# A gated cross-attention block with routed experts on one core: a projection's products spread between an attention slot's scores

## The chip, the cores and the metric

The kernel runs on one core of a Trainium2 chip, as one launch. The metric is the device time in microseconds. Before the change three runs took 877.08, 871.36 and 870.76 us (median 871.36 us).

## The reference

`x` is (8, 256, 512), eight batches of 256 tokens; `ctx` has the same shape. Everything is float32. Cut to what matters:

```
h  = layernorm(x)
q  = concat(ctx, h) @ Wq                      # 32 heads of 16
k  = h @ Wk ; v = h @ Wv ; sk = ctx @ Wsk ; sv = ctx @ Wsv      # 8 key heads of 16
scores = q @ concat(sk, k)^T / 4 + alibi,  banded to 64 keys back, softmax
x  = x + tanh(g0) * (softmax(scores) @ concat(sv, v)) @ Wo
h2 = layernorm(x)
x  = x + tanh(g1) * (routed experts of h2, top 4 of 128, mixed from 8 bases, + a shared expert)
```

The attention is 256 units of work: 8 batches, 8 key heads, 4 blocks of 64 queries. A unit's scores are computed twice: once with queries as rows, for the maxima of the softmax, and once turned, with keys as rows, for the probabilities that multiply the values.

## The kernel before

Each product of two float32 matrices is made of three fp32r products (high times high, low times high, high times low). The splitting into high and low parts is done by ScalarE (ACT, the high part) and then by VectorE (DVE) or GpSimd (POOL), the low part.

**Slots.** PE's program for the attention is a loop over slots, `for n in range(SLOTS)`, written out by hand. A batch has 32 slots, and "slot 24" here means n mod 32 = 24. In slot n PE does, in this order:

- `scores(n)` (L1944): two products with 114 rows, `ps_scores<-k_stack,q_stack`, of 192 columns each, or of 128 each in every fourth unit. DVE reduces them to maxima (`neg_max`, L1490). Before it starts, the unit two slots back must have been reduced (semaphore `max_done`).
- in every eighth slot `times_v` (L1987, 64 instructions on PE with a 32-column weight load each), in another of eight `turn_max` (L1962), a turning of the maxima.
- `scores_turned(n - 18)` (L1973): two products with 116 rows and 256 columns, `ps_scoresT<-q_stack,k_stack` (one in every fourth unit). ACT takes the exponentials (`probsT`, L1128). Before it starts, the unit two slots back must be through ACT (`exp_done`).
- turnings of normalised rows, in some slots.
- **a piece of a projection** for a later batch, in 24 of a batch's 32 slots: a third of a key, value or query projection (8 products of 128 rows and 256 columns) or of an output projection `times_wo` (4 products of 128 rows and 512 columns). In the first eight slots it is an eighth of a query projection (3 products).
- in the last batches and behind them: router, gate and up products of the expert part.

Which slot has which piece comes from tables at the top: `K_PROJ`, `V_PROJ`, `Q_PROJ`, `EARLY_Q` and `TIMES_WO`. Over the whole loop 167 slots have a piece: 18 of keys, 21 of values, 86 of queries (8 of them of three products), 42 of the output. The output projection of a batch starts in slot 24 of the next batch (batches 0 to 5), that of batch 6 in slot 25 of the last one.

**Waits around a piece.** The first product of a projection waits until its PSUM bank has been emptied (`take_bank`, `pj_done`). For the output projection it waits for more: `oT_lo`, the low part of the attention's output. That comes about so: `times_v` on PE; DVE turns and inverts; POOL multiplies; DVE turns back (`oT_raw`); ACT makes `oT_hi` (L1139); POOL makes `oT_lo` (L847). The last `oT_hi` of a batch stands in ACT's order directly behind the exponentials of slot 22, and slot 22 has the last third of a value projection.

ACT, DVE and POOL work through lists of their own, each strictly in order.

## Time and profile before

| | |
|---|---|
| runs | 877.08, 871.36, 870.76 us |
| the profiled execution: time | 872.62 us |
| its span | 870.6 us |
| PE busy | 858.4 us, 99% of the span |
| weight loads (PEld) busy | 753.4 us, 87% |
| DVE, POOL, ACT busy | 545.2, 519.9, 399.3 us |
| granted TensorE clock | 1.00 in every stretch asked for |
| chain that ended last | PE 84%, POOL 10%, DMA 2%, DVE 2% |

PE is TensorE's matmuls, PEld its weight loads, which have a row of their own. The profile models where a matmul ends, and consecutive matmuls overlap in it, so the distance between starts is what a product costs. The attention runs from about 34 us to about 400 us; the shared and routed experts follow and end the program.

### The profile page before, as it was taken

The page shows a single profiled execution, that of the slowest core. Times are in us where ns is not written, and L with a number is a line of the kernel's source. Part 1 is how long each engine was busy: PE and PEld are TensorE (multiplying, and loading weights), DVE is VectorE, ACT ScalarE, POOL GpSimd, SP SyncE. Part 2 cuts the span into 40 slices and gives each one's busy share as a digit, 9 for nine tenths or more (in the row PEclk, how much of TensorE's full clock was granted, in tenths as well). Part 3 has the DMA queues.
Part 4 walks back from the last instruction along what each step waited for, and adds up shares of the span by engine and source line. Part 5 has one row for each costly group of instructions (what it writes and reads, how often), then busy time and mean ns, then how long its engine had stood idle before and what let it go on. Part 6 is the DMA issues. An engine that isn't in the chain of part 4 may idle for free.

```text
span 870.6 us, 17391 instructions
## 1 busy us (share of the span) xinstructions
PE 858.4 (99%) x6662; PEld 753.4 (87%) x6662; DVE 545.2 (63%) x984; ACT 399.3 (46%) x807; POOL 519.9 (60%) x532
## 2 busy tenths in 40 slices
PE   9899999999999999999999999999999999999998
PEld 8889999999999998988888877888888888888886
DVE  7675666766666657756446756556655655665567
ACT  5754545554545544655035243444444444444431
POOL 3861443535335232343769998548888887888641
PEclk9999999999999999999999999999999999999999
DMA  8678676776868659630101354320212022021046
GB/s 275 170 143 180 152 207 186 191 196 167 205 165 218 163 139 256 144 100 25 49 25 49 102 168 157 134 73 25 82 40 73 25 72 73 25 84 38 1 151 236
DMA packets 76509, 108.09 MB, mean 124 GB/s; under 512 B 7274, under 2 KB 47979, under 8 KB 75403
## 3 DMA queue, kind: packets, MB, share of 16 engines
q1 hardware_dynamic: 74168, 105.94, 43.4%
q10 hardware_dynamic: 2258, 1.03, 0.5%
q8 instruction: 54, 0.88, 0.5%
q14 instruction: 29, 0.23, 0.1%
HBM read 70.71 MB, written 31.00 MB: 117 GB/s over the span
## 4 chain that ended last, share of the span: by engine, by line
PE 84%; POOL 10%; DMA 2%; DVE 2%; issue 1%; SPq 1%; ACT 0%; POOLq 0%; ACTq 0%
PE ps_scores L2227 20%; PE ps_proj L1846 15%; PE ps_scoresT L2227 10%; PE ps_scoresT L1983 7%; PE ps_o L1997 6%; PE ps_scores L1956 5%; PE ps_proj L2227 5%; PE ps_proj L1904 5%; PE ps_scores L1846 3%; PE ps_proj L1835 3%; PE ps_scoresT L1846 1%; DMA q_stack<-max_rows 1%; POOL sum_lo L953 1%; POOL sum_raw L968 1%; POOL sum_raw L966 1%; DMA xn_rows<-in_x 1%
## 5 line engine op out<-in xcount | busy, mean ns | idle before, releaser
L1128 ACT ACTIVATE probsT<-ps_scoresT 128x512 f32<-128x512 f32 (+1 forms) x256 | 138.9, 545 | 148.9 <-PE ps_scoresT L1983 144.4
L1490 DVE TENSOR_REDUCE neg_max<-ps_scores 128x2 f32<-128x384 f32 (+1 forms) x256 | 131.6, 516 | 108.6 <-PE ps_scores L1956 107.8
L1357 ACT ACTIVATE part_sums<-ps_scores 128x512 f32<-128x512 f32 x96 | 57.4, 598 | 130.1 <-PE ps_scores L2227 130.0
L1983 PE MATMUL ps_scoresT<-q_stack,k_stack 116*128 116x256 f32 x448 | 106.1, 307 | 0.8 <-DMA q_stack<-max_rows 0.8
L841 POOL TENSOR_TENSOR o_normal<-o_blocks,inv_sums 128x256 f32<-128x256 f32 x32 | 19.9, 622 | 138.0 <-DVE inv_sums L1511 138.0
L1956 PE MATMUL ps_scores<-k_stack,q_stack 114*128 114x192 f32 (+1 forms) x512 | 94.5, 267 | 2.7 <-DMA q_stack<-qT_hi 1.6
L1956 PEld LDWEIGHTS ps_scores<-k_stack,q_stack 114*128 114x128 f32 x512 | 83.0, 190 | 9.5 <-DMA q_stack<-qT_hi 2.3
L996 POOL TENSOR_TENSOR w_expert_lo<-w_sums,w_expert_hi 128x256 fp32r<-128x256 f32 x64 | 64.2, 1014 | 44.9 <-ACT w_expert_hi L1277 44.9
L1008 POOL TENSOR_TENSOR big<-big,basis 128x512 f32<-128x512 f32 x56 | 77.9, 1409 | 16.3 <-DVE basis L1785 16.3
L1983 PEld LDWEIGHTS ps_scoresT<-q_stack,k_stack 116*128 116x128 f32 x448 | 70.8, 190 | 4.7 <-DMA q_stack<-max_rows 1.0
L1776 DVE TENSOR_TENSOR basis<-part_sums,silu_gate 128x512 f32<-128x512 f32 x32 | 24.2, 755 | 67.3 <-ACT silu_gate L1365 67.3
L1846 PE MATMUL ps_proj<-actT_hi,wq_hi 128*128 128x256 f32 x224 | 63.6, 284 | 0.5 <-DVE second_qT_lo L1467 0.5
L1846 PE MATMUL ps_proj<-actT_lo,wq_hi 128*128 128x256 f32 x224 | 63.3, 282 | 0.0
L1846 PE MATMUL ps_proj<-actT_hi,wq_lo 128*128 128x256 f32 x224 | 63.3, 282 | 0.0
L847 POOL TENSOR_TENSOR oT_lo<-oT_raw,oT_hi 128x256 fp32r<-128x256 f32 x32 | 23.6, 737 | 59.0 <-ACT oT_hi L1139 59.0
L1785 DVE TENSOR_TENSOR basis<-basis,big 128x512 f32<-128x512 f32 x56 | 56.8, 1015 | 1.0
L1997 PE MATMUL ps_o<-probsT,v_ones 128*32 128x128 f32 (+1 forms) x2048 | 55.7, 261 | 0.0
L1755 DVE TENSOR_TENSOR part_sums<-part_sums,ps_scoresT 128x512 f32<-128x512 f32 x32 | 22.0, 687 | 53.4 <-ACT part_sums L1357 53.4
L1997 PEld LDWEIGHTS ps_o<-probsT,v_ones 128*32 128x32 f32 x2048 | 50.5, 110 | 4.0 <-issue 1.1
L996 POOL TENSOR_TENSOR w_expert_lo<-w_raw,w_expert_hi 128x256 fp32r<-128x256 f32 x48 | 46.4, 980 | 6.9 <-ACT w_expert_hi L1277 6.8
L2227 PE MATMUL ps_scores<-xnT_hi,w_expert_hi 128*128 128x512 f32 x128 | 49.8, 389 | 0.0
L2227 PE MATMUL ps_scores<-xnT_hi,w_expert_lo 128*128 128x512 f32 x128 | 49.8, 389 | 0.0
(309 smaller groups left out, 2500.9 us busy)
## 6 DMA issues: line engine op xcount, KB each, us to landing
k_stack<-k_kept SPq DMA_DIRECT2D x64, 192.0 KB, 4.3
big<-coeff_rows SPq DMA_DIRECT2D x8, 1024.0 KB, 4.8
q_stack<-q_kept SPq DMA_DIRECT2D x40, 192.0 KB, 4.1
q_kept<-qT_hi SPq DMA_DIRECT2D x10, 512.0 KB
x_rows<-in_x SPq DMA_DIRECT2D x9, 512.0 KB, 5.8
k_kept<-kT_hi SPq DMA_DIRECT2D x16, 256.0 KB
x_kept<-x_rows SPq DMA_DIRECT2D x16, 256.0 KB, 2.6
w_raw<-in_L_ffn_w_gate SPq DMA_DIRECT2D x16, 256.0 KB, 2.8
```

The lines of the kernel that those rows point to most:

```text
L996: pool.tensor_tensor(WS[n % 2]["lo"][:, w, :], w_source(n, w), WS[n % 2]["hi"][:, w, :].bitcast(F32), ALU.subtract).then_inc(e_lo, 1)
L1008: pool.tensor_tensor(dst, dst, BS[:, j, :], ALU.add).then_inc(acc_done, 1)
L1128: act.activation(PT[:, g % 2, 2 * j:2 * j + blocks].rearrange("p h f r w -> p (h f r w)"), ST[:, n % 2, 0:blocks].rearrange("p h n -> p (h ...
L1357: act.activation(TP[:, u % 2, j, :], src[:, u % 2, :], ACT.Copy).then_inc(taken, 1)
L1490: dve.tensor_reduce(NM[:, g // 2 % 2, g % 2, 2 * i:2 * i + 2], SA[:, n % 2, :, 0:keys], AX.X, ALU.max, negate=True).then_inc(max_done, 1)
L1785: dve.tensor_tensor(dst, BS[:, j, :], cB[:, k % 2, group_columns(t)], ALU.mult).then_inc(basis_done, 1)
L1846: ins = pe.matmul(out, stat(s, c), mov(m, c), start=i == 0, stop=i == len(steps) - 1, skip_group_check=True)
L1904: ins = pe.matmul(dst[:, src * T:(src + 1) * T], WKV[w][:, m + src, c, :], AT[x][:, src * HC + c, :], start=i == 0, stop=i == HC * PARTS - ...
L1956: ins = pe.matmul(SA[:, n % 2, f, 0:2 * (near.stop - near.start)], QS[0:TOP, g, i, f].rearrange("p r w -> p (r w)"), keys[:, near, :].rear ...
L1983: ins = pe.matmul(ST[:, n % 2, v, :], KS[0:ROWS, g, j + v, 1 - v].rearrange("p w s -> p (w s)"), QS[0:ROWS, g, j + v].rearrange("p f r w - ...
L1997: ins = pe.matmul(POB[32 * r:32 * r + 2 * D, n % 2, j * W:j * W + cols_j], VA[:, j, n % HK, :], PT[:, n % 2, 2 * j:2 * j + cols_j // W, :, ...
L2227: ins = pe.matmul(bank[:, u % 2, :], WS[n % 2][s][:, w, c * P:(c + 1) * P], operand(MEETS[w], m, c, g), start=first and c == 0 and j == 0, ...
```

## The change

The piece of a projection no longer stands behind the slot's scores as one block. `scores` and `scores_turned` each do one of their two products per call, and a new function `projected(n, cut)` does a part of the slot's piece: its first product between the two score products, its second before the turned scores, its third between the two turned ones, and the rest where the piece stood before. Slots without a piece keep their order. Nothing is added or taken away, and the lists of ACT, DVE, POOL and SyncE stay as they are.

```diff
-        def third(out, stat, mov, count, part, pieces=3):
+        def third(out, stat, mov, count, part, done, pieces=3, cut=WHOLE):
             steps = [(c, s, m) for c in range(count) for s, m in PASSES]
             size = len(steps) // pieces
-            for i in range(part * size, (part + 1) * size) if part is not None else range(len(steps)):
+            piece = range(part * size, (part + 1) * size) if part is not None else range(len(steps))
+            for i in piece[cut]:
                 c, s, m = steps[i]
                 ins = pe.matmul(out, stat(s, c), mov(m, c), start=i == 0, stop=i == len(steps) - 1, skip_group_check=True)
-            return ins
+                if i == len(steps) - 1:
+                    ins.then_inc(done, 1)
...
-        def times_wo(b, t, part):
-            first = part in (0, None)
+        def times_wo(b, t, part, cut=WHOLE):
+            first = part in (0, None) and cut.start == 0
             dst = take_bank("wo", b, t) if first else place("wo", b, t)
             if first:
                 pe.wait_ge(oT_lo, HC * (b + 1))
                 banks_back(b)
-            ins = third(dst, lambda h, c: OT[h][:, t, c, :], lambda h, c: WO[h][:, c, :], HC, part)
-            if part in (2, None):
-                ins.then_inc(wo_mm, 1)
+            third(dst, lambda h, c: OT[h][:, t, c, :], lambda h, c: WO[h][:, c, :], HC, part, wo_mm, cut=cut)
...
+        def projected(n, cut):
+            if n < PIECES:
+                queries(1, 1, n, PIECES, cut)
+            for part in range(3):
+                b = due(n, K_PROJ[part], 2)
+                if b is not None:
+                    keys_values_third("k", b, part, cut)
...
         for n in range(SLOTS):
             if n < END:
-                scores(n)
+                scores(n, 0)
+            projected(n, slice(0, 1))
+            if n < END:
+                scores(n, 1)
             p = pair_due(n, PV)
             if p is not None:
                 times_v(p)
             p = pair_due(n, NM_TURN)
             if p is not None:
                 turn_max(p)
+            projected(n, slice(1, 2))
             if LAG <= n < END + LAG:
-                scores_turned(n - LAG)
+                scores_turned(n - LAG, 0)
+            projected(n, slice(2, 3))
+            if LAG <= n < END + LAG:
+                scores_turned(n - LAG, 1)
...
+            projected(n, slice(3, None))
```

The waits stand at the same products as before, `max_done` at a slot's first score product and `exp_done` at its first turned one; the semaphores that tell that a pair is done are raised by the second. In the rows below `ps_proj` is the projection's bank, and what stands in brackets is what the instruction waits for.

PE in slot 22, the last third of a value projection, before:

```order
L1956 MATMUL ps_scores<-k_stack,q_stack 128x192 [waits max_done]
L1956 MATMUL ps_scores<-k_stack,q_stack 128x192
L1983 MATMUL ps_scoresT<-q_stack,k_stack 128x256 [waits exp_done]
L1983 MATMUL ps_scoresT<-q_stack,k_stack 128x256
L1904 MATMUL ps_proj<-actT_hi,wkv_lo 128x256
L1904 MATMUL ps_proj<-actT_lo,wkv_hi 128x256
```

and now:

```order
L1957 MATMUL ps_scores<-k_stack,q_stack 128x192 [waits max_done]
L1907 MATMUL ps_proj<-actT_hi,wkv_lo 128x256
L1957 MATMUL ps_scores<-k_stack,q_stack 128x192
L1907 MATMUL ps_proj<-actT_lo,wkv_hi 128x256
L1986 MATMUL ps_scoresT<-q_stack,k_stack 128x256 [waits exp_done]
L1907 MATMUL ps_proj<-actT_hi,wkv_hi 128x256
L1986 MATMUL ps_scoresT<-q_stack,k_stack 128x256
L1907 MATMUL ps_proj<-actT_hi,wkv_lo 128x256
L1907 MATMUL ps_proj<-actT_lo,wkv_hi 128x256
```

The second turned product now stands behind three products of the piece; five instead of eight follow it.

PE in slot 24, where an output projection starts, before:

```order
L1956 MATMUL ps_scores<-k_stack,q_stack 128x128 [waits max_done,q_in6,stack_in6]
L1956 MATMUL ps_scores<-k_stack,q_stack 128x128
L1983 MATMUL ps_scoresT<-q_stack,k_stack 128x256 [waits exp_done]
L1983 MATMUL ps_scoresT<-q_stack,k_stack 128x256
L1846 MATMUL ps_proj<-wo_hi,oT_hi 128x512 [waits oT_lo,pj_done]
L1846 MATMUL ps_proj<-wo_hi,oT_lo 128x512
```

and now:

```order
L1957 MATMUL ps_scores<-k_stack,q_stack 128x128 [waits max_done,q_in6,stack_in6]
L1848 MATMUL ps_proj<-wo_hi,oT_hi 128x512 [waits oT_lo,pj_done]
L1957 MATMUL ps_scores<-k_stack,q_stack 128x128
L1848 MATMUL ps_proj<-wo_hi,oT_lo 128x512
L1986 MATMUL ps_scoresT<-q_stack,k_stack 128x256 [waits exp_done]
L1848 MATMUL ps_proj<-wo_lo,oT_hi 128x512
L1986 MATMUL ps_scoresT<-q_stack,k_stack 128x256
L1848 MATMUL ps_proj<-wo_hi,oT_hi 128x512
```

The product that waits for `oT_lo` has moved ahead of three of the slot's four score products.

## Rows read from the trace of the kernel before

**Rows 1.** Stretch (us), busy of PE, PEld, DVE, ACT, POOL, granted clock, DMA share, GB/s.

```profile
200.00:300.00 100.00, 100.00 (x1185) 95.84 (x1184) 70.28 (x161) 52.26 (x108) 43.02 (x56) 1.00 0.74 190
```

**Rows 2.** Waits of PE, the longest in total: us, times, longest.

```profile
PE ps_scores L1956 <- DMA q_stack<-qT_hi: 1.6, 3, 0.6
```

**Rows 3.** Timeline, weight loads (PEld), one slot: start us, us, instruction.

```profile
303.37 0.31 PEld L1956 LDWEIGHTS ps_scores<-k_stack,q_stack 114*128 114x128 f32 x2
...
303.60 0.30 PEld L1983 LDWEIGHTS ps_scoresT<-q_stack,k_stack 116*128 116x128 f32 x2
...
303.83 0.19 PEld L1846 LDWEIGHTS ps_proj<-actT_hi,wq_hi 128*128 128x128 f32 x1
...
304.79 0.31 PEld L1956 LDWEIGHTS ps_scores<-k_stack,q_stack 114*128 114x128 f32 x2
```

**Rows 4.** Timeline, matmuls (PE) of two score pairs.

```profile
303.49 0.37 PE L1956 MATMUL ps_scores<-k_stack,q_stack 114*128 114x192 f32 x2
...
304.78 0.28 PE L1846 MATMUL ps_proj<-actT_hi,wq_lo 128*128 128x256 f32 x1
...
304.90 0.34 PE L1956 MATMUL ps_scores<-k_stack,q_stack 114*128 114x128 f32 x2
```

**Rows 5.** Timeline, the end of slot 22 and slot 24 of one batch.

```profile
144.12 0.30 PEld L1983 LDWEIGHTS ps_scoresT<-q_stack,k_stack 116*128 116x128 f32 x2
...
144.67 0.60 ACT L1128 ACTIVATE probsT<-ps_scoresT 128x512 f32<-128x512 f32 x1 [0.24 <-PE ps_scoresT L1983]
...
145.17 0.41 ACT L1139 ACTIVATE oT_hi<-oT_raw 128x256 fp32r<-128x256 f32 x1
...
145.65 0.74 POOL L847 TENSOR_TENSOR oT_lo<-oT_raw,oT_hi 128x256 fp32r<-128x256 f32 x1 [2.68 <-ACT oT_hi L1139]
...
146.22 0.30 PEld L1956 LDWEIGHTS ps_scores<-k_stack,q_stack 114*128 114x128 f32 x2
...
146.68 0.19 PEld L1846 LDWEIGHTS ps_proj<-wo_hi,oT_hi 128*128 128x128 f32 x1
```

**Rows 6.** Timeline, the first such place.

```profile
99.19 0.73 POOL L847 TENSOR_TENSOR oT_lo<-oT_raw,oT_hi 128x256 fp32r<-128x256 f32 x1 [2.78 <-ACT oT_hi L1139]
...
99.66 0.30 PEld L1956 LDWEIGHTS ps_scores<-k_stack,q_stack 114*128 114x128 f32 x2
```

**Rows 7.** Timeline, the last such place.

```profile
330.99 0.73 POOL L847 TENSOR_TENSOR oT_lo<-oT_raw,oT_hi 128x256 fp32r<-128x256 f32 x1 [2.69 <-ACT oT_hi L1139]
...
331.56 0.30 PEld L1956 LDWEIGHTS ps_scores<-k_stack,q_stack 114*128 114x128 f32 x2
```

**Rows 8.** Timeline, a projection whose first load waits for POOL.

```profile
63.57 1.28 POOL L834 TENSOR_TENSOR actT_lo<-ctx_turned,actT_hi 128x512 fp32r<-128x512 f32 x1
...
64.96 0.19 PEld L1904 LDWEIGHTS ps_proj<-actT_hi,wkv_hi 128*128 128x128 f32 x1
```

**Rows 9.** Timeline, slot 9 of the first batch.

```profile
41.37 0.41 DVE L1467 TENSOR_TENSOR second_qT_lo<-ps_proj,second_qT_hi 128x256 fp32r<-128x256 f32 x1
...
41.84 0.19 PEld L1846 LDWEIGHTS ps_proj<-actT_hi,wq_hi 128*128 128x128 f32 x1 [0.72 <-DVE second_qT_lo L1467]
```

**Rows 10.** Timeline, slot 25 of the last batch.

```profile
371.35 0.30 PEld L1956 LDWEIGHTS ps_scores<-k_stack,q_stack 114*128 114x128 f32 x2
...
371.49 0.59 ACT L1157 ACTIVATE logitsT<-ps_proj 128x512 f32<-128x512 f32 x1
...
372.08 0.09 PEld L1971 LDWEIGHTS ps_scoresT<-ident,max_halves 128*32 128x32 f32 x1 [0.43 <-DVE max_halves L1500]
...
372.28 0.19 PEld L1846 LDWEIGHTS ps_proj<-wo_hi,oT_hi 128*128 128x128 f32 x1
...
373.08 0.43 PEld L1956 LDWEIGHTS ps_scores<-k_stack,q_stack 114*128 114x128 f32 x2
```

**Rows 11.** Timeline, a close wait of a turned score.

```profile
233.71 0.60 ACT L1128 ACTIVATE probsT<-ps_scoresT 128x512 f32<-128x512 f32 x1 [1.92 <-PE ps_scoresT L1983]
...
234.53 0.30 PEld L1983 LDWEIGHTS ps_scoresT<-q_stack,k_stack 116*128 116x128 f32 x2
```

More of the change, by code:

```diff
@@ L78 @@
 LAG = 18
+WHOLE = slice(0, None)
 PAIR = 2 * NB
@@ L2105, in _ @@
         queries(1, 0, 1, 2)
+        def projected(n, cut):
[5 more added lines that the diff above has]
+                    keys_values_third("k", b, part, cut)
+                for r in range(G):
+                    b = queries_due(n, r, part)
+                    if b is not None and (b > 1 or r > 1):
+                        queries(b, r, part, cut=cut)
+                b = due(n, V_PROJ[part], 1)
+                if b is not None:
+                    keys_values_third("v", b, part, cut)
+                for t in range(TB):
+                    b = wo_due(n, t, part)
+                    if b is not None:
+                        if b == 0 and t == 0 and part == 0 and cut.start == 0:
+                            for m in range(FIRST_O, len(halves)):
+                                wait_split(pe, m)
+                        times_wo(b, t, part, cut)
         for n in range(SLOTS):
             if n < END:
-                scores(n)
+                scores(n, 0)
+            projected(n, slice(0, 1))
+            if n < END:
+                scores(n, 1)
             p = pair_due(n, PV)
```

81 lines of the change are left out of this document (28 added, 53 removed).

## The prediction

> **What bounds the kernel now.** I read the share of busy time first: PE is busy for 858.4 of 870.6 us. Then the stretches. From 200 to 300 us, in the middle of the attention, PE has no idle time at all and the granted clock is 1.00, that is 2.4 GHz, while the next engine, DVE, is at 70% [rows 1]. Then PE's own waits: the longest in total is 1.6 us in three waits, for the first loads of the query stack [rows 2], and all its other waits are shorter in total. So the attention is bound by the number of products on PE and by what each costs there. Time is gained only if a product becomes cheaper; it is lost wherever PE is made to wait, since nothing later gives it back.
>
> What a product costs is read from the starts of the weight loads, since the profile models the ends of matmuls. In one slot the loads of two scores, two turned scores and eight projection products start at 303.37, 303.49, 303.60, 303.71 and 303.83, and those of the next slot at 304.79 (a merged pair's second start is its end less 0.19) [rows 3]. A load starts with the matmul before it, so the cost of one shows one place late: 303.60 - 303.49 and 303.71 - 303.60 are the two scores, 0.11 us each, 303.83 - 303.71 a turned product, 0.12, and (304.79 - 303.83) / 8 a projection product, 0.12: 2 x 0.11 + 2 x 0.12 + 8 x 0.12 = 1.42 us, which is 304.79 - 303.37.
>
> **The order alone: 0.** In 167 slots the same products change places. The score product is the only one whose columns need less than its cost: its pair starts 0.09 us apart with 192 columns and 0.06 with 128 (0.37 and 0.34 less 0.28, the length of a single matmul) [rows 4], yet the loads behind it are 0.11 apart [rows 3]. So what a score costs is the weight load of whatever comes next, and a projection product's load is the same 0.19 us long. I take each product's cost to be its own, whoever its neighbours are: the sum above has three changes of kind in it and nothing left over. Bounds: it could save 0.02 us per wide score and 0.05 per narrow one, or lose what a reading can hide, 0.01 us per change of kind; both are rivals below. I take 0 because the sum of the twelve closes with nothing over.
>
> The Trainium skill, "TensorE: Matmul & The Clock Gate", on what happens when a matmul is issued, says that the next tile's weights load while this tile's matmul runs. Taken alone it speaks for the change: a wide product beside a narrow one hides its load. The trace agrees only that far, that the load starts with the matmul before it, and its 0.11 us stand behind a 0.06 us matmul; by the rule the sum would be the first rival's, by the row it is 0.
>
> **What moves earlier and waits.** The first product of a piece is now second in its slot, ahead of one score and two turned ones: 0.11 + 0.12 + 0.12 = 0.35 us earlier. Query, key and value pieces wait there only for a bank emptied microseconds ago; PE shows no wait at them in the stretch without idle [rows 1]. The output projection waits for `oT_lo`, and there it is tight. **What moves later** is the second turned product, by three products, 0.36 us, and with it ACT's exponentials. In slot 22 they start at 144.67, directly behind their release, ACT having been idle; `oT_hi` follows at 145.17 directly behind them, and `oT_lo` on POOL, which had waited 2.68 us, from 145.65 to 146.39 [rows 5]. All three move by 0.36 us, since none had slack: `oT_lo` ends at 146.75. Slot 22 holds the last third of a value projection in all six batches concerned. In slot 24 the scores' load starts at 146.22, the output product could load at 146.33, and before loaded at 146.68 [rows 5]. What such a wait takes from POOL's end to the load is seen elsewhere: `actT_lo` ends at 64.85 and the load starts at 64.96, 0.11 us [rows 8]. So the load starts at 146.75 + 0.11 = 146.86, and PE waits 0.53 us. In the first such place POOL ends at 99.92 and the scores load at 99.66: 99.92 + 0.36 + 0.11 - 99.77 = 0.62 [rows 6]. In the last it is 331.72 + 0.47 - 331.67 = 0.52 [rows 7]. Four more lie between, like the one shown: 0.62 + 4 x 0.53 + 0.52 = **3.3 us**. Bounds per place: 0.17 us if `oT_lo` does not move, 0.53 if all of it does; I take the second because ACT and POOL both stood waiting.
>
> **Two smaller places.** In slot 9 of the first batch the piece waits for DVE's `second_qT_lo`, which ends at 41.78; the load follows at 41.84 [rows 9]. A score product (0.11) and the turning of the maxima (0.09, the length of its load [rows 10]) were done inside that wait and now come behind it: +0.2 us. In slot 25 of the last batch the output projection also waits for ACT's `logitsT`, which ends at 372.08, so it loads at 372.19. Behind it now come four output products (0.80, from 372.28 to 373.08 before) and three that had been ahead, 0.11 + 0.09 + 0.12: slot 26 starts at 373.31 instead of 373.08 [rows 10]: +0.2 us.
>
> **What gets more room.** The first turned product of a slot moves 0.24 us later, or more behind output products. Its closest wait in the steady part is in slot 20, where ACT ends at 234.31 and the load starts at 234.53 [rows 11]; it gains distance. But there was no wait there, so that is worth nothing. The longest waits, for DMAs of the query stack, stand at a slot's first score, which stays first.
>
> **Sum.** 3.3 + 0.2 + 0.2 = 3.7 us. Against the profiled execution's 872.62 us that gives 876.3. It stands 1.3 us over the median of the runs; against the median, 871.36, the forecast is **875.1 us**, 0.4% slower. The expert part gives little back: it runs on PE too, and no wait of PE as long as the longest one [rows 2] stands there.
>
> **Rivals.**
> 1. *Loads are hidden.* A score between two wide products costs only its columns: 0.02 us saved for each score in three of four units and 0.05 in the fourth, times two, times 167: 9.2 us. With the waits it is 9.2 - 3.7 = 5.5 us faster, 865.9; without them 862.2. For it: the load starts with the matmul before, and that is now a wide one. Against: it is the load behind the score that costs, and that one cannot start before the score does. Chance 0.10.
> 2. *The change does nothing to be seen.* The order costs nothing and `oT_lo` comes in time, because ACT's exponentials or POOL have slack that the trace hides, or what is lost at the output is won in the waits of the first and last batch: 871.4. For it: PE is idle for 870.6 - 858.4 = 12.2 us in all, and some of its waits now have products beside them. Against: the longest stand at a slot's first score [rows 2], which nothing of the slot can precede. Chance 0.17.
> 3. *Changing the height of the operands costs* (slower). Scores use 114 rows, turned ones 116, projections 128. A piece slot had three changes of height and now has eight: 5 x 167 = 835 more. At 0.01 us, the most that the intervals can hide, 8.4 us, and with the waits 12.1: 883.5. It passes 1% from 0.006 us a change. For it: no row shows a turned product directly behind a projection product. Against: the sum of twelve closes with three such changes in it. Chance 0.13.
>
> **Numbers.** The forecast has 0.60. About 1% (8.7 us) is what a measurement of this kernel can tell from no change; the three runs shown are 6.3 us apart. Over 1% faster is only the far end of rival 1, 0.04; over 1% slower is rival 3 and a little of the forecast's upper tail, 0.12; within 1%: 0.84. The range is 870.0 to 880.5: it takes in rival 2 with a microsecond of scatter, the forecast, and rival 3 with a price of up to 0.006 us, and leaves out rival 1 and the rest of rival 3.
>
> **What would show it.** PE's waits should have a new line, an output product waiting for POOL's `oT_lo`, six times with about 0.4 to 0.6 us each (less in that view, which counts from the modelled end of the matmul before). The slot of rows 3 should still take 1.42 us from its first load to the next slot's; 1.37 would be rival 1, 1.47 rival 3. The exponentials of slot 22 should start 0.36 us later after the slot's start than now. From the first such place to the last, five batches, 331.56 - 99.66 = 231.9 us pass now [rows 6, 7]; it should be 2.7 us more, 234.6. The prediction is wrong if no such wait stands in slot 24, or if the slots without it have a new length.

## Result, and the profile after

| | before | changed |
|---|---|---|
| median | 871.30 us (15 runs, 870.51 to 877.08) | 877.02 us (15 runs, 875.96 to 881.30) |
| ratio, 95% interval | | 1.007, 1.0057 to 1.0083 |
| profiled execution, span | 872.62, 870.6 us | 875.96, 873.9 us |

The change costs 5.7 us, 0.7%; 3.7 were forecast. The waits forecast are there in their places and sizes, and a small price that the prediction put at zero comes on top.

**The stretch without idle.** The changed kernel, same stretch and columns as [rows 1]:

```profile
200.00:300.00 100.00, 99.34 (x1183) 94.86 (x1176) 68.23 (x154) 51.38 (x107) 41.87 (x55) 1.00 0.70 183
```

PE was busy for 100.00 us here and now is for 99.34, at the same granted clock of 1.00: it waits.

**PE's waits.** The lines of the changed kernel's list (us in total, times, longest) that name one of the three places, and the DMA line of [rows 2]:

```profile
PE ps_proj L1848 <- POOL oT_lo L848: 2.1, 6, 0.4
PE ps_scores L1957 <- DMA q_stack<-qT_hi: 1.6, 3, 0.9
...
PE ps_proj L1848 <- DVE second_qT_lo L1468: 0.7, 1, 0.7
...
PE ps_proj L1848 <- ACT logitsT L1158: 0.5, 1, 0.5
```

An output product waits for `oT_lo` six times and has taken the top of the list. Before, neither the first nor the last of these lines was there. The view counts from the modelled end of the matmul before, so 2.1 us is less than the loss, as the prediction had said.

**Slots 22 and 24**, the same batch as [rows 5]: timeline of the changed kernel, start us, us, instruction, in brackets the idle time before it and its releaser.

```profile
146.38 0.60 ACT L1129 ACTIVATE probsT<-ps_scoresT 128x512 f32<-128x512 f32 x1 [0.61 <-PE ps_scoresT L1986]
...
146.88 0.41 ACT L1140 ACTIVATE oT_hi<-oT_raw 128x256 fp32r<-128x256 f32 x1
...
147.36 0.73 POOL L848 TENSOR_TENSOR oT_lo<-oT_raw,oT_hi 128x256 fp32r<-128x256 f32 x1 [3.06 <-ACT oT_hi L1140]
147.58 0.19 PEld L1957 LDWEIGHTS ps_scores<-k_stack,q_stack 114*128 114x128 f32 x1
...
148.21 0.19 PEld L1848 LDWEIGHTS ps_proj<-wo_hi,oT_hi 128*128 128x128 f32 x1 [0.44 <-issue]
```

Against slot 24's first load, the exponentials of slot 22 start 1.20 us ahead now (147.58 - 146.38) and did 1.55 us ahead before (146.22 - 144.67): 0.35 us later, forecast 0.36. `oT_hi` follows directly, `oT_lo` ends at 148.09, and 0.12 us behind that the output product loads. With no wait it would load one score product after 147.58, at 147.69, and loads at 148.21: 0.52 us lost, forecast 0.53.

The first and the last such place, as [rows 6] and [rows 7]:

```profile
100.04 0.73 POOL L848 TENSOR_TENSOR oT_lo<-oT_raw,oT_hi 128x256 fp32r<-128x256 f32 x1 [3.17 <-ACT oT_hi L1140]
100.17 0.19 PEld L1957 LDWEIGHTS ps_scores<-k_stack,q_stack 114*128 114x128 f32 x1
...
100.89 0.18 PEld L1848 LDWEIGHTS ps_proj<-wo_hi,oT_hi 128*128 128x128 f32 x1 [0.53 <-issue]
...
335.70 0.73 POOL L848 TENSOR_TENSOR oT_lo<-oT_raw,oT_hi 128x256 fp32r<-128x256 f32 x1 [3.08 <-ACT oT_hi L1140]
...
335.91 0.19 PEld L1957 LDWEIGHTS ps_scores<-k_stack,q_stack 114*128 114x128 f32 x1
...
336.54 0.19 PEld L1848 LDWEIGHTS ps_proj<-wo_hi,oT_hi 128*128 128x128 f32 x1 [0.44 <-issue]
```

The same reading gives 100.89 - 100.17 - 0.11 = 0.61 us and 336.54 - 335.91 - 0.11 = 0.52 us (forecast 0.62 and 0.52). From the first such place to the last, 235.74 us pass, and 231.90 before: 3.84 more, not 2.7. The waits are 2.7 of it (0.61 + 4 x 0.52). So something stands between the places.

**The slot of [rows 3].** Its first load and the next slot's in the changed kernel:

```profile
307.58 0.19 PEld L1957 LDWEIGHTS ps_scores<-k_stack,q_stack 114*128 114x128 f32 x1
...
309.01 0.19 PEld L1957 LDWEIGHTS ps_scores<-k_stack,q_stack 114*128 114x128 f32 x1
```

1.43 us, where 1.42 stood. That is at the edge of what two rows show. Over many slots it is not. I took the start of all 256 slots from both traces and subtracted their lengths. In ns, the fourth batch:

```
slots  0 to  7    1  18  -1  17   7   1  12  19
slots  8 to 15    8   3  -1  13   4  -1  -2   7
slots 16 to 23    3  17   0  -1   6  15  13   1
slots 24 to 31  517  11   5  12  15  -4   9  24
```

Slots without a piece (2, 9, 10, 13, 14, 18, 19, 23) keep their length within 3 ns. Those with one are longer by 10 ns on average, slot 24 left out, and by nearly the same amounts in each batch, slot by slot. Leaving slot 24 out, the six batches from the second to the seventh are longer by 258, 229, 231, 228, 231 and 229 ns: 1.4 us in all.

**The two smaller places**, slot 9 of the first batch as [rows 9], and slot 25 of the last as [rows 10]:

```profile
41.45 0.41 DVE L1468 TENSOR_TENSOR second_qT_lo<-ps_proj,second_qT_hi 128x256 fp32r<-128x256 f32 x1
41.91 0.19 PEld L1848 LDWEIGHTS ps_proj<-actT_hi,wq_hi 128*128 128x128 f32 x1 [0.88 <-DVE second_qT_lo L1468]
...
375.40 0.19 PEld L1957 LDWEIGHTS ps_scores<-k_stack,q_stack 114*128 114x128 f32 x1
...
375.54 0.59 ACT L1158 ACTIVATE logitsT<-ps_proj 128x512 f32<-128x512 f32 x1
...
376.25 0.19 PEld L1848 LDWEIGHTS ps_proj<-wo_hi,oT_hi 128*128 128x128 f32 x1 [0.66 <-issue]
...
377.38 0.43 PEld L1957 LDWEIGHTS ps_scores<-k_stack,q_stack 114*128 114x128 f32 x2
```

In slot 9 the load still follows DVE by 0.05 us, and the score and the turning now come behind it: the slot is 0.20 us longer, as forecast. In slot 25 ACT's `logitsT` ends at 376.13 and the load starts at 376.25; the slot takes 1.98 us instead of 1.73: 0.25, forecast 0.2.

**A wait that only the profile of before had.** Weight loads in the slot behind `times_v` at the start of the last batch, first before, then changed:

```profile
347.89 0.30 PEld L1983 LDWEIGHTS ps_scoresT<-q_stack,k_stack 116*128 116x128 f32 x2 [1.00 <-DMA q_stack<-max_rows]
```

```profile
351.92 0.30 PEld L1986 LDWEIGHTS ps_scoresT<-q_stack,k_stack 116*128 116x128 f32 x2
```

Before, PE had idled for 1.00 us for a DMA of the maxima; the changed kernel's execution has no such wait, and its slot is 0.89 us shorter. Whether that is scatter of one execution is not shown. Both profiles of before's order (before, e6) have the wait, all three of the full spread order (changed, e10, e5) lack it, and of the other experiments' profiles some have it and some don't. The budget below gives it apart.

**Budget of the two traces**, from the first slot's start to the last one's: 3.20 (six slots 24) + 0.20 + 0.25 + 1.41 (other slots with a piece, six batches) - 0.89 (the DMA wait) - 0.10 (the rest) = 4.07 us. Without that DMA wait it is 5.0.

### The profile page after: what moved, and what is told of

The parts are those of the page before. It is cut to its first block, busy times and chain, and to the rows that moved or that the text cites. A ratio compares the mean times of both kernels' runs of the same rounds, so it can differ in the third digit from the quotient of the medians.

```text
span 873.9 us, 17391 instructions
## 1 busy us (share of the span) xinstructions
PE 860.7 (98%) x6662; PEld 755.5 (86%) x6662; DVE 546.3 (63%) x984; ACT 398.1 (46%) x807; POOL 520.2 (60%) x532
## 4 chain that ended last, share of the span: by engine, by line
PE 81%; POOL 10%; issue 3%; DVE 3%; DMA 1%; ACT 1%; SPq 0%; POOLq 0%; DVEq 0%; ACTq 0%
PE ps_scores L2235 20%; PE ps_proj L1848 16%; PE ps_scoresT L2235 10%; PE ps_o L2001 6%; PE ps_scoresT L1986 6%; PE ps_proj L2235 5%; PE ps_scores L1957 4%; PE ps_proj L1907 3%; PE ps_scores L1848 3%; PE ps_proj L1836 3%; PE ps_scoresT L1848 1%; POOL sum_lo L954 1%; POOL sum_raw L969 1%; POOL sum_raw L967 1%; DMA xn_rows<-in_x 1%
## 5 line engine op out<-in xcount | busy, mean ns | idle before, releaser
L1957 PE MATMUL ps_scores<-k_stack,q_stack 114*128 114x192 f32 (+1 forms) x512 | 115.3, 258 | 2.7 <-DMA q_stack<-qT_hi 1.6
L1986 PE MATMUL ps_scoresT<-q_stack,k_stack 116*128 116x256 f32 x448 | 115.6, 295 | 0.0
L1957 PEld LDWEIGHTS ps_scores<-k_stack,q_stack 114*128 114x128 f32 x512 | 92.9, 191 | 6.9 <-DMA q_stack<-qT_hi 2.2
L1986 PEld LDWEIGHTS ps_scoresT<-q_stack,k_stack 116*128 116x128 f32 x448 | 80.0, 191 | 3.7
L1848 PE MATMUL ps_proj<-actT_hi,wq_hi 128*128 128x256 f32 x224 | 65.5, 292 | 0.7 <-DVE second_qT_lo L1468 0.7
L1848 PE MATMUL ps_proj<-actT_lo,wq_hi 128*128 128x256 f32 x224 | 65.4, 292 | 0.0
L1848 PE MATMUL ps_proj<-actT_hi,wq_lo 128*128 128x256 f32 x224 | 65.1, 291 | 0.0
L2235 PE MATMUL ps_scores<-xnT_lo,w_expert_hi 128*128 128x512 f32 x128 | 49.9, 390 | 0.0
```

Of the source, the lines that this page charges most:

```text
L1848: ins = pe.matmul(out, stat(s, c), mov(m, c), start=i == 0, stop=i == len(steps) - 1, skip_group_check=True)
L1957: ins = pe.matmul(SA[:, n % 2, f, 0:2 * (near.stop - near.start)], QS[0:TOP, g, i, f].rearrange("p r w -> p (r w)"), keys[:, near, :].rear ...
L1986: ins = pe.matmul(ST[:, n % 2, v, :], KS[0:ROWS, g, j + v, 1 - v].rearrange("p w s -> p (w s)"), QS[0:ROWS, g, j + v].rearrange("p f r w - ...
L2235: ins = pe.matmul(bank[:, u % 2, :], WS[n % 2][s][:, w, c * P:(c + 1) * P], operand(MEETS[w], m, c, g), start=first and c == 0 and j == 0, ...
```

## Experiments

One view decides between most theories. The distance from slot 24 of the third batch to slot 24 of the seventh is 185.34 us before [rows 5, 7] and has no waits of the start, the end or the DMA in it. It holds four places where `oT_lo` may be waited for and four batches of other slots. All were measured against before on the same chip.

| run | what it is | ratio, 95% interval | median, before | oT_lo, each of four | four batches, more than before |
|---|---|---|---|---|---|
| changed | | 1.007 (1.0057 to 1.0083) | 877.02, 871.30 | 0.52 | 2.99 |
| e1 | output pieces behind | 1.0048 (1.0028 to 1.0069) | 875.42, 871.95 | 0.17 | 1.31 |
| e2 | only output pieces spread | 1.0018 (1.0008 to 1.0028) | 873.72, 871.95 | 0.17 | 0.77 |
| e3 | as e1, slot 22's value piece behind | 1.0026 (1.0008 to 1.0044) | 874.30, 871.95 | 0 | 0.59 |
| e4 | oT_hi ahead of exponentials | 1.0024 (1.0008 to 1.0039) | 873.92, 871.95 | 0 | 0.96 |
| e5 | changed, all heights 114 | 1.0051 (1.0027 to 1.0074) | 876.62, 871.97 | 0.53 | 1.78 over e6 |
| e6 | before, all heights 114 | 1.0009 (0.9992 to 1.0025) | 871.92, 871.97 | 0 | 0.11 |
| e7 | only the two scores taken apart | 1.0042 (1.0025 to 1.0058) | 875.25, 871.97 | 0.28 | 1.57 |
| e8 | only the two turned ones apart | 1.0011 (0.9997 to 1.0025) | 873.05, 871.97 | 0.07 | 0.63 |
| e9 | changed, products of slots 0 to 33 behind | 1.006 (1.0039 to 1.0081) | 877.78, 871.68 | 0.52 | 3.01 |
| e10 | changed, again | 1.0057 (1.0036 to 1.0079) | 877.62, 871.68 | 0.52 | 3.02 |
| e11 | as e4 and e9, slot 25 of the last batch | 1.0035 (1.0021 to 1.0049) | 875.16, 871.68 | 0 | 0.96 |
| e12 | e11 without the moved waits | 1.0026 (1.0012 to 1.004) | 873.52, 871.97 | 0 | 0.96 |

**Which half of the wait is which: e1, e2, e3.** A wait for `oT_lo` has two causes, the product that moved ahead (slot 24) and the exponentials that moved back (slot 22). In e1 output pieces stay behind:

```diff
                 for t in range(TB):
-                    b = wo_due(n, t, part)
+                    b = wo_due(n, t, part) if cut.start == 3 else None
                     if b is not None:
...
-                        times_wo(b, t, part, cut)
+                        times_wo(b, t, part)
```

> The changed kernel with the output projection's pieces back behind the slot's scores; key, value and query pieces stay spread. Theory A (the loss is the wait for oT_lo, made of the product moved 0.35 us earlier and of oT_lo coming 0.36 us later, plus a price of about 9 ns a slot for the alternation): oT_lo still comes 0.36 us late, so a wait of about 0.18 us stays in five of the six places and 0.28 in the first, 1.2 us in place of 3.2; the alternation in the other 125 slots costs 1.1, slot 9 0.2: 2.5 us over the kernel before. Rival B (the wait comes from the earlier place alone): no wait for oT_lo at all, 1.3 us over. Rival C (the waits are given back later, and the loss is the alternation's): as slow as the changed kernel, 5 us over.

e2 is its mirror:

```diff
-            if n < PIECES:
+            wo_cut, cut = cut, (WHOLE if cut.start == 3 else slice(0, 0))
+            if n < PIECES and cut == WHOLE:
...
-                b = due(n, K_PROJ[part], 2)
+                b = due(n, K_PROJ[part], 2) if cut == WHOLE else None
...
-                        times_wo(b, t, part, cut)
+                        times_wo(b, t, part, wo_cut)
```

> Only the output projection's pieces are spread; key, value and query pieces stand behind the scores as before the change. Theory A: oT_lo comes as early as before the change, so the product moved 0.35 us ahead waits about 0.17 us in five places and 0.26 in the first, 1.1 us in all; slot 25 of the last batch costs 0.2, the alternation in 42 slots 0.4: 1.7 us over the kernel before. Rival B (the earlier place alone): the whole 3.2 us of waits, 3.9 us over. Rival C: 0.4 over.

e3 is e1 with the last third of a value projection (slot 22) whole as well:

```diff
-                if b is not None:
-                    keys_values_third("v", b, part, cut)
+                if b is not None and (part < 2 or cut.start == 3):
+                    keys_values_third("v", b, part, cut if part < 2 else WHOLE)
```

> As e1, and the last third of the value projection, in slot 22, also behind its scores. Theory A: oT_lo is on time and nothing asks for it earlier: no wait for it; what stays is the alternation in 118 slots, about 1.1 us, and slot 9, 0.2: 1.3 us over the kernel before, 1.2 under e1. Rival B: the same as its e1, as slot 22 doesn't matter.

Either half alone gives 0.17 us per place, both give 0.52, and without both it is 0 (slot 24 is 0 to 3 ns longer than before in e3). 0.17 + 0.17 is less than 0.52, because before the change `oT_lo` was early: in [rows 5] it ends at 146.39 and the product loads at 146.68, so, with the 0.11 us from POOL's end to the load, the first 0.18 us of either delay cost nothing. This is what the prediction's two bounds of 0.17 and 0.53 said. In the runs e1 and e3 stand further off than expected, e1 at +3.5 us for +2.5, e3 at +2.3 for +1.3; e2 is as expected. The last part of this section takes that up.

**Taking the wait away by ACT's order: e4.** The change stays whole; ACT makes a batch's last `oT_hi` ahead of slot 22's exponentials, which no longer delay it:

```diff
+            p = split_due(n)
+            if p is not None and p % HC == HC - 1:
+                o_high(p)
             if LAG <= n < END + LAG:
                 exponentials(n - LAG)
...
             p = split_due(n)
-            if p is not None:
+            if p is not None and p % HC < HC - 1:
                 o_high(p)
```

> The changed kernel with one step of ACT's list moved: the last oT_hi of a batch stands ahead of slot 22's exponentials instead of behind them. Theory A: the delay of the second turned product no longer reaches oT_lo, which ends about 0.7 us earlier than in the kernel before: all six waits for oT_lo go, 3.2 us under the changed kernel, 2.0 over the one before. Rival B' (POOL or DVE sets when oT_lo comes): the waits stay, no change against the changed kernel.

The same place in e4's timeline:

```profile
147.01 0.40 ACT L1140 ACTIVATE oT_hi<-oT_raw 128x256 fp32r<-128x256 f32 x1
...
147.49 0.74 POOL L848 TENSOR_TENSOR oT_lo<-oT_raw,oT_hi 128x256 fp32r<-128x256 f32 x1 [1.86 <-ACT oT_hi L1140]
...
147.72 0.60 ACT L1129 ACTIVATE probsT<-ps_scoresT 128x512 f32<-128x512 f32 x1 [0.30 <-PE ps_scoresT L1989]
...
148.92 0.19 PEld L1960 LDWEIGHTS ps_scores<-k_stack,q_stack 114*128 114x128 f32 x1
...
149.03 0.19 PEld L1851 LDWEIGHTS ps_proj<-wo_hi,oT_hi 128*128 128x128 f32 x1
```

`oT_lo` ends at 148.23, 0.8 us before the output product loads. That load comes 0.11 us behind the score's, with no wait; all six places are like this. e4 came out at +2.0 us as expected. It is the changed kernel's loss less the waits.

**Why slots with a piece are longer: e5 to e8.** Rival 3 had the height of the operands as its cause. In e5 and e6 every one of these products has 114 rows:

```diff
-                ins = pe.matmul(dst[:, src * T:(src + 1) * T], WKV[w][:, m + src, c, :], AT[x][:, src * HC + c, :],
+                ins = pe.matmul(dst[:, src * T:(src + 1) * T], WKV[w][0:TOP, m + src, c, :], AT[x][0:TOP, src * HC + c, :],
...
-                ins = pe.matmul(ST[:, n % 2, v, :], KS[0:ROWS, g, j + v, 1 - v].rearrange("p w s -> p (w s)"),
-                                QS[0:ROWS, g, j + v].rearrange("p f r w -> p (f r w)"), start=True, stop=True)
+                ins = pe.matmul(ST[:, n % 2, v, :], KS[0:TOP, g, j + v, 1 - v].rearrange("p w s -> p (w s)"),
+                                QS[0:TOP, g, j + v].rearrange("p f r w -> p (f r w)"), start=True, stop=True)
```

(and in the same way for query and output projections). Both kernels leave 14 of 128 terms out of every projection and the maxima out of the turned scores.

> The changed order with all operands of scores, turned scores and projections cut to 114 rows, so that no change of height is left between them. It leaves the maxima out of the turned scores and 14 of 128 terms out of every projection. To be read against e6, slot by slot. Theory H (the alternation's price, 8 to 23 ns in most slots with a piece, is that of changing height): slots of e5 are as long as those of e6, the waits aside. Rival L (it belongs to the alternation itself: another bank, another buffer): the same 5 to 23 ns stay.

> The order of the kernel before with the same cut to 114 rows; the same terms are left out. Both theories: as long as the kernel before within 0.5 us, since the height of an operand does not set how long its columns take.

The two loads that bound the four batches (slots 24 of the third and the seventh), first e6, then e5:

```profile
147.60 0.30 PEld L1956 LDWEIGHTS ps_scores<-k_stack,q_stack 114*128 114x128 f32 x2
...
333.05 0.30 PEld L1956 LDWEIGHTS ps_scores<-k_stack,q_stack 114*128 114x128 f32 x2
```

```profile
148.22 0.19 PEld L1957 LDWEIGHTS ps_scores<-k_stack,q_stack 114*128 114x128 f32 x1
...
335.45 0.19 PEld L1957 LDWEIGHTS ps_scores<-k_stack,q_stack 114*128 114x128 f32 x1
```

185.45 us and 187.23 us: 1.78 more. Four waits in slot 24 are 2.14 of it, so everything else is 0.36 us *shorter* with the products spread, where it was 0.92 us longer with unequal heights (2.99 - 4 x 0.517). In the fourth batch slots with a piece are from 16 ns shorter to 12 ns longer in e5 than in e6, nearly all of them shorter or equal. So the spread order costs something only where the heights are unequal. At equal heights it shows a small gain, some 4 ns a slot with a piece, in the direction of rival 1 at a thirteenth of its size (0.09 us a batch; it had 9.2 us over the eight). The runs are too coarse for either: e5's median is 4.7 us over e6's.

The other half of the comparison is e6 against before: the old order with the heights made equal, all changes of height between these products gone. Its four batches are 0.11 us *longer* than before's. A fixed price for each change of height would have made them shorter, by about 0.8 us at 2.2 ns each (my estimate from three changes in each of 24 slots and two in each of the other 8). So what costs is unequal heights in the spread order; the old order pays nothing for them.

e7 and e8 split the change by pair. e7 takes only the score products apart, e8 only the turned ones:

```diff
# e7
             projected(n, slice(0, 1))
...
-            projected(n, slice(1, 2))
             if LAG <= n < END + LAG:
                 scores_turned(n - LAG, 0)
-            projected(n, slice(2, 3))
...
-            projected(n, slice(3, None))
+            projected(n, slice(1, None))
```

> Only the two score products are taken apart: the first product of a piece between them, the rest behind the turned scores as before the change. Every piece's first product still moves 0.35 us earlier, the second turned product comes 0.12 us later. Theory A: a wait for oT_lo of 0.17 + 0.12 = 0.29 us in five places, 0.38 in the first, 1.8 us in all; slots get longer by what a projection product ahead of a single score costs. Theory P (the price sits at the turned pair, where the trace of the changed kernel shows 122 ns for a projection product ahead of a turned one and 121 ahead of a score, against 119): 1 to 3 ns a slot here and 3 to 8 in e8. Rival (it sits at the scores): the reverse.

```diff
# e8
-            projected(n, slice(0, 1))
...
-            projected(n, slice(1, 2))
             if LAG <= n < END + LAG:
                 scores_turned(n - LAG, 0)
-            projected(n, slice(2, 3))
+            projected(n, slice(0, 1))
...
-            projected(n, slice(3, None))
+            projected(n, slice(1, None))
```

> Only the two turned products are taken apart: the first product of a piece between them, the rest behind. The second turned product comes 0.12 us later, the first product of a piece 0.12 us earlier. Theory A: the product that waits for oT_lo is ready 0.12 us earlier and oT_lo comes 0.12 us later, against 0.18 us that are free after the 0.11 us a wait takes: waits of 0.06 us in five places and 0.15 in the first, 0.5 us in all; no cost in slot 9 beyond nothing, since no turned product stands there. Theory P: slots with a piece 3 to 8 ns longer.

Outside slot 24 a batch is 0.11 us longer in e7 and 0.10 in e8, against 0.23 in the changed kernel. The idea that the price sits mainly at the turned pair fell: each half of the change has about half of it. Does it go by the number of changes of height? A steady batch has 23 slots with a piece beside slot 24, 17 with two turned products and 6 with one. The changed kernel adds 17 x 5 + 6 x 3 = 103 changes a batch, e7 23 x 2 = 46, e8 17 x 2 = 34: 2.2, 2.4 and 2.9 ns each. By batch that looks like a rate. Slot by slot it is none: in the changed kernel the slots that gain three changes are 9.7 ns longer and those that gain five 10.2, and in e8 the six slots that gain none are still 3.3 ns longer, for 4.7 in the others. In e2, where only output pieces are spread, it is 28 ns a batch for 21 changes, 1.3 ns each. What the price goes by stays open.

The loads say where it lies. A projection product with a single score behind it takes 121 ns, and one with a single turned product 122, for 119 in before (means over the steady batches, from load to load). In e5 both still take 121. What equal heights take away lies at other products: in e5 a score with a projection product and a turned one behind it takes 109 ns, for 111 in the changed kernel, and a turned product with a projection product behind it 117 to 119, for 120 to 121. So it is not the step between two heights alone that costs.

The waits for `oT_lo` came as expected, 0.28 us in e7 (the output product 0.35 us earlier, the second turned one 0.12 later, less the 0.18 of room) and 0.07 in e8 (0.12 and 0.12, less 0.18; its slot 24 is 0.05 us longer).

**Why the runs stand further off than the traces: e9 to e12.** For each run a mean granted clock is listed. Of the changed kernel's 15 runs the five at 1.000 lie at 875.96 to 876.90 us and the nine at 0.998 or less at 876.90 to 881.30 (one more has 0.999); their medians are 876.44 and 879.36. e10 repeats the changed kernel as it is; e9 was meant to keep the first batch as before:

```diff
         def projected(n, cut):
+            if n < 34:
+                cut = WHOLE if cut.start == 3 else slice(0, 0)
```

> The changed kernel, with the pieces of slots 0 to 33 left as a block behind the slot's scores; everything else spread. Open is why the runs of the changed kernel (median 5.7 us over before) stand further off than the two traces (5.2 us without one DMA wait). The runs list a mean granted clock each: of the changed kernel's 15, five have 1.000 and lie at 875.96 to 876.90 us, the other ten have 0.995 to 0.999 and lie at 876.90 to 881.30; three experiments' profiles show the clock at 0.50 for 3.41 us from 65 to 66 us, in slot 31 of the first batch, at some 1.4 us. Theory C, the spread order of the first batch makes such a fall likelier: with the first batch as before, falls are as rare as before (runs at 0.998 or less: none to two of ten), and the median is the changed kernel's less 0.2 us (slot 9) less 0.1 (changes of height in the first batch) less about 1: 875.5, +4.7 against 870.8 to 872. Theory N, the fall has nothing to do with the order in the first batch but with the run or the chip: it is as frequent here as in the changed kernel on the same chip, and the median is only 0.3 us under it. In the trace both give: slots 0 to 33 within 0.05 us of before but for scatter of waits, oT_lo waits six times, end of the attention about 4.9 us later than before's less 0.9 where that DMA wait is missing.

> The changed kernel as it is, on the same chip as its neighbours here, for their comparison and for how often the granted clock falls. Expected: ratio 1.0066, +5.0 to +6.2 us; five to seven of ten runs with a mean clock of 0.998 or less, which are 1 to 4 us over those at 1.000; those at 1.000 stand 4.9 us over before's runs at 1.000, since the two traces differ by 5.2 us on TensorE but for one DMA wait. In the trace: oT_lo waits six times, 3.2 us in all; 230 ns a batch in the other slots with a piece.

e10's profile caught such a fall. Columns: stretch, busy of PE, PEld, DVE, ACT, POOL, granted clock, DMA share, GB/s:

```profile
63.00:65.00 2.00, 1.24 (x6) 0.89 (x6) 1.97 (x5) 1.30 (x3) 2.00 (x3) 1.00 0.58 101
65.05:68.40 3.35, 3.35 (x17) 3.35 (x18) 1.23 (x4) 0.60 (x1) 0.96 (x1) 0.50 0.77 180
68.50:71.00 2.50, 2.50 (x26) 2.40 (x28) 0.56 (x1) 1.59 (x5) 0.73 (x1) 1.00 0.38 62
```

and before in the first two stretches:

```profile
63.00:65.00 2.00, 1.50 (x9) 1.15 (x9) 2.00 (x6) 1.36 (x3) 2.00 (x3) 1.00 0.73 142
65.05:68.40 3.35, 3.14 (x25) 2.94 (x26) 1.74 (x5) 1.50 (x3) 1.31 (x2) 1.00 0.76 172
```

The clock, third column from the end, is 0.50 from 65.05 to 68.40, that is 1.2 GHz, behind a stretch in which PE was busy for 1.24 of 2.00 us. PE does 17 matmul rows there where before does 25, and the two slots there, 31 of the first batch and 0 of the second, are longer than before's by 0.78 and 0.63 us. The profiles of e1, e3 and e4 have the same fall, from 65.0, 65.5 and 66.4 us on, for 3.41 us, in the same two slots, at the same cost of 1.4 us. With the runs at 1.000 alone e1 is 2.8 us over before (expected 2.5) and e3, with three such runs, 0.5 (expected 1.3), so the falls can account for what these two had over their expectation.

What stands just ahead of it are three waits of PE. Weight loads with idle time before them, e10:

```profile
63.18 0.30 PEld L1957 LDWEIGHTS ps_scores<-k_stack,q_stack 114*128 114x128 f32 x2 [0.49 <-DVE neg_max L1491]
...
64.23 0.19 PEld L1957 LDWEIGHTS ps_scores<-k_stack,q_stack 114*128 114x128 f32 x1 [0.46 <-DVE neg_max L1491]
...
64.89 0.19 PEld L1907 LDWEIGHTS ps_proj<-actT_hi,wkv_hi 128*128 128x128 f32 x1 [0.47 <-issue]
```

and before:

```profile
63.24 0.30 PEld L1956 LDWEIGHTS ps_scores<-k_stack,q_stack 114*128 114x128 f32 x2 [0.49 <-DVE neg_max L1490]
...
64.30 0.30 PEld L1956 LDWEIGHTS ps_scores<-k_stack,q_stack 114*128 114x128 f32 x2 [0.46 <-DVE neg_max L1490]
...
66.14 0.19 PEld L1904 LDWEIGHTS ps_proj<-actT_hi,wkv_hi 128*128 128x128 f32 x1 [0.41 <-POOL actT_lo L834]
```

The third wait, for POOL's `actT_lo`, belongs to the piece. Spread, it comes behind one score product, 0.66 us after the second wait; as a block it comes 1.84 us after. About the same idle time lies closer together. But that alone does not bring the fall. The changed kernel's first profile has the same three waits, 1.06 and 0.66 us apart, PE no busier there, and its clock stays at 1.00:

```profile
63.40:65.40 2.00, 1.24 (x6) 0.89 (x7) 1.97 (x5) 1.29 (x3) 2.00 (x3) 1.00 0.73 170
```

And the fall has another place too. In e11's profile it comes at the start of the attention, behind one long wait for a DMA, where the products stand as in before, and the first five slots are 0.8 us longer. The wait, and the stretch of the fall:

```profile
35.51 0.30 PEld L1960 LDWEIGHTS ps_scores<-k_stack,q_stack 114*128 114x128 f32 x2 [2.02 <-DMA q_stack<-qT_hi]
```

```profile
36.35:39.76 3.41, 3.41 (x19) 3.41 (x18) 1.73 (x4) 3.38 (x8) 3.41 (x4) 0.50 0.59 112
```

e10 itself answers against the clock as the whole cause. It came within its +5.0 to +6.2 us, at +6.0, with three of six runs at 0.998, but these (877.61 to 877.73) are no slower than the others: its three runs at 1.000 have a median of 877.54, 5.9 us over before's runs at 1.000, where 4.9 were expected.

e9 missed its 875.5 us: 877.78, no better than e10, though one run in seven only had 0.998 or less. That too speaks against the clock as the whole cause. Its edit did less than meant. The empty first part of a piece still waited at the changed place, so slot 9 was still 0.22 us longer, and only the products went back. e11 has the same fault:

```diff
         def projected(n, cut):
+            if n < 34 or n == 249:
+                cut = WHOLE if cut.start == 3 else slice(0, 0)
```

on top of e4's edit.

> The changed kernel with all three of its new waits taken out and the spreading kept in all other slots: ACT's last oT_hi of a batch ahead of slot 22's exponentials (no wait for oT_lo), the pieces of slots 0 to 33 as blocks behind the scores (slot 9), and the piece of slot 25 of the last batch too. What is left are the changes of height, 0.23 us in each of six batches, and a few in the last. My theory (2 to 2.5 ns per change, nothing else): slots with a piece longer as in the changed kernel, slot 24 +5 ns, slot 25 of the last batch 0; in all +1.4 us against before, ratio 1.0016. The theory that the order alone gives something back once nothing waits (the first rival of the prediction, or 'nothing seen'): 0 or under, ratio 1.0000 or less. The theory that there is another loss in the order: +3 us or more at a mean clock of 1.000.

In the runs e11 is 3.5 us over before, and 2.8 with those at 1.000 alone, for +1.4. In its trace slot 25 of the last batch came out 0.61 us longer instead of 0 and slot 9 0.22; the clock's fall shown above is another 0.8, and a longer DMA wait ahead of slot 0 1.1. e12 is the version meant, which leaves TensorE's program up to slot 33 as before:

```diff
+            if n < 34 or n == 249:
+                if cut.start < 3:
+                    return
+                cut = WHOLE
```

> The kernel that the expectation of e11 meant, now with nothing of a piece, its waits included, ahead of the scores in slots 0 to 33 and in slot 25 of the last batch (in e11, as in e9, an empty first part of the piece still waited at the changed place, so that slot 9 stayed +0.2 us and slot 25 of the last batch became +0.6). ACT's last oT_hi of a batch goes ahead of slot 22's exponentials. TensorE's program up to slot 33 is that of before. My theory: in the trace slots 0 to 33 differ only by scatter, slot 9 by 0 to 0.02 us; slot 24 +5 ns; other slots with a piece 230 to 240 ns a batch; slot 25 of the last batch within 0.02 us; no wait for oT_lo, logitsT or earlier second_qT_lo. In all +1.4 us, ratio 1.0016, 872.4 to 873.8 at 871.7 for before. If the clock's falls around 65 us come from the first batch's order, they are as rare as before's (runs at 0.998 or less: two of 18 in the last set, none to two of ten here) and the runs at 1.000 and all runs have the same median; if not, three to six of ten have them, and the median is another microsecond over. If the order gives anything back once nothing waits: ratio 1.0000 or under.

The loads that bound the four batches in e12:

```profile
146.25 0.19 PEld L1960 LDWEIGHTS ps_scores<-k_stack,q_stack 114*128 114x128 f32 x1
...
146.36 0.19 PEld L1851 LDWEIGHTS ps_proj<-wo_hi,oT_hi 128*128 128x128 f32 x1
...
332.55 0.19 PEld L1960 LDWEIGHTS ps_scores<-k_stack,q_stack 114*128 114x128 f32 x1
```

The output product loads 0.11 us behind the score, and 186.30 us pass: 0.96 more than before, 0.24 a batch. From the first slot to the last, e12's trace is 1.12 us longer than before's, with the DMA wait of before in both. Slot 25 of the last batch is 0.09 us shorter, where within 0.02 was expected. 873.52 against 871.97 is +1.55 us, forecast +1.4; the interval is 1.0 to 3.5 us, and the runs at 1.000 alone give +0.7. So the small price remains when all three waits are gone, and the order gives nothing back. No version beat the kernel before: of those that compute the same, the two that differ least are e8, 1.0011, whose interval includes 1, and e2, 1.0018.

How often the clock fell (runs with a mean of 0.998 or less; they do not tell where): with the key piece's wait ahead of the second score, 12 of 21 in the changed kernel (with e10) and 22 of 48 in e1, e3, e4, e5 and e7; with that wait as late as before, 8 of 96 in before, 1 of 18 in e2 and e8, 8 of 31 in e9, e11 and e12. That points to the closer waits, but e6, with before's order, had 5 of 10, and e7 1 of 8. It stays open what decides it in a single run, and so does how much of the changed kernel's distance it makes.

## Why the prediction was right, and where it was short

**Forecast: slower by 0.4%, within 1%.** Measured 0.7%, 877.0 us in a range of 870.0 to 880.5. It was the likeliest case, with its mechanism.

- *What moves earlier and waits, 3.3 us.* Right: 0.61 + 5 x 0.52 = 3.2 us. Both halves are shown apart (e1, e2), together (changed, e9, e10), and gone (e3; e4, e11 and e12 by the other road). The bound of 0.17 us per place for `oT_lo` not moving is what e2 measured.
- *Slot 9, 0.2 us.* Right, 0.20. *Slot 25, 0.2 us.* 0.25.
- *What gets more room: nothing.* Right in the steady batches. In the first batch slots 3 and 7 are 0.18 us shorter each and slots 2 and 6 0.09 longer, in all 0.17 us that the prediction did not have.
- *The order alone, 0.* This is the term that was mis-sized. It measured 1.4 us, 0.23 a batch. The prediction argued that the sum of the twelve products closes with nothing left over. That sum could not have failed to close: all its terms are distances between the same loads, and the projection product's 0.12 is what was left of the slot, divided by eight. It also comes from a slot in the old order, and the rows of before have no single score between two projection products; so it says nothing of what the new order costs. The text had the right bound, 0.01 us per change, and in rival 3 the right condition, unequal heights, but priced that rival only at 0.01. With its 835 changes even 2 ns each would have been 1.7 us, nearly half of the forecast. The law of rival 3, a price for each change, is not borne out (e6, and the slots with three and with five), and its count was too high: a slot with one turned product gains three changes, not five. By the prediction's own last sign, that it is wrong if slots without the wait have a new length, this term failed: they have one, by 10 ns.
- *A score costs its own 0.11 us, whoever its neighbours are.* Held to within the price above: a first or single score takes 0.111 us in both kernels, from load to load. So rival 1, which by the Trainium skill ("TensorE: Matmul & The Clock Gate", on what happens when a matmul is issued) has the next weights loaded under the running product, gave no 9 us; what the equal heights of e5 and e6 show of it is 0.09 us a batch. The same page says, in its section on LDWEIGHTS, that a weight load's time goes by its columns and not by its rows. The trace agrees for the single load, 0.19 us long with 114, 116 and 128 rows. It does not carry over to a sequence: e5 is shorter than the changed kernel, by 0.28 us a batch outside slot 24, by its rows alone.
- *Rival 2, nothing to be seen.* Wrong: the six waits are there, and e12 shows that nothing comes back once they are gone.
- *The sum.* 3.7 was forecast, and 3.20 + 0.20 + 0.25 + 1.41 = 5.1 us found. The changed kernel's five runs at a clock of 1.000 fit that: 876.44 against a median of 871.30 before. e10's three do not: 877.54 against 871.67, 5.9 us. The rest up to 5.7 is in part the clock's fall, which more of the changed kernel's runs have than of before's; that it is all of it is not shown. So 1.4 us of the order and some 0.6 us beyond the traces were not foreseen. The signs to look for came out as 0.35 us later for 0.36, 1.43 us for 1.42, and 3.84 for 2.7 us between the places; the last one alone told that something had been left out.

## What to carry to other kernels

On an engine that never idles, moving an instruction is paid for at each end: ask what waits for the one that moves back, through how many engines it goes on, and whether the one that moves ahead can start. Give a term "0" only after multiplying the reading error by the count: 10 ns is nothing in one slot and 1.4 us over a kernel, and a distance over several batches resolves it where single rows don't. A sum whose last term is the remainder always closes, and shows nothing. Spreading products of unequal height among each other had a price here that equal heights did not have; but equal heights alone, in the old order, gained nothing. And test such a price in both orders: that equal heights take it away in one does not make it a price of each change.

## What the runs showed of the hardware

- Spreading products of 128 rows among products of 114 and 116 rows costs 0.23 us a batch, 10 ns a slot with a piece; with 114 rows everywhere the same spreading gains 0.09 (e5 against e6), and in the old order equal rows gain nothing (e6 against before: 0.03 us a batch longer). It is not a fixed price per change of rows. What in the engine causes it no run shows.
- The granted clock fell to 0.50 for 3.41 us, at about 65 us behind short waits (e1, e3, e4, e10), at 1.4 us each, or at 36.35 us behind a DMA wait of 2.02 us (e11), in some executions and not in others of the same program: the changed kernel's first profile has no fall, its second has.
- A product that waits for POOL's `oT_lo` loads 0.11 to 0.12 us behind POOL's end (336.43 to 336.54, 100.77 to 100.89); one that waits for DVE's `second_qT_lo` loads 0.05 us behind it (41.86 to 41.91) in the same kernel.
